# Convolution heads in three passes on high and low halves, with products made ahead in the attention and kept in DRAM

## What is computed

```
x = x + linear_attention(layernorm(x))
# convolution, 32 heads of 8 channels; q = layernorm(x), k = v = ctx
kv  = einsum('bhil,bhjl->bijhl', k_, v_)
y   = irfft(rfft(kv, 2L) * rfft(ssm_kernel, 2L))[..., :L]
out = y + kv * D[None, None, None, :, None]
x = x + einsum('bijhl,bhil->bjhl', out, q_)
x = x + experts(layernorm(x)) + shared_expert(layernorm(x))
```

## Time and profile before

| what | us |
|---|---|
| median of three runs (lowest, highest) | 864.95 (864.42, 866.53) |
| the profiled execution | 864.47 |
| its span, first to last instruction | 861.4 |
| PE busy in the span | 841.6 (98%) |
| DVE, ACT, POOL busy | 544.6, 377.5, 443.2 |
| PE busy from 100 to 140 us (attention) | 39.88 of 40 |
| PE busy from 280 to 320 us (convolution) | 40.00 of 40 |
| POOL busy in the same two stretches | 13.83, 36.52 |

### The profile page before, as it was taken

One profiled execution on the slowest core, in us unless ns is written; L12 is line 12 of the kernel. 1 busy time (PEld: TensorE's weight loads), 2 busy tenths in 40 slices (PEclk: granted clock), 3 DMA queues, 4 the chain that ended last, 5 costly groups with the idle time before them and its releaser, 6 DMA issues.

```text
span 861.4 us, 14213 instructions
## 1 busy us (share of the span) xinstructions
PE 841.6 (98%) x4354; PEld 702.5 (82%) x4354; DVE 544.6 (63%) x850; ACT 377.5 (44%) x608; POOL 443.2 (51%) x436
## 2 busy tenths in 40 slices
PE   8999999999999999999999999999999999999995
PEld 7888888889877777778887788888888888888884
DVE  5767767675657777888769875544455544555431
ACT  5313322333133533442652255555655555655552
POOL 1203223331068899884622343666666666656654
PEclk9999999999999999999999999999999999999998
DMA  8601101100026543440210297988899888999866
GB/s 284 218 25 17 34 24 37 37 12 13 1 62 197 165 129 110 123 132 16 93 63 7 92 322 188 213 207 212 192 190 215 210 210 197 190 199 217 207 120 87
DMA packets 54420, 113.42 MB, mean 132 GB/s; under 512 B 10416, under 2 KB 14256, under 8 KB 54256
## 3 DMA queue, kind: packets, MB, share of 16 engines
q1 hardware_dynamic: 37360, 72.49, 26.3%
q0 software_dynamic: 17024, 40.48, 25.2%
HBM read 82.28 MB, written 30.66 MB: 131 GB/s over the span
## 4 chain that ended last, share of the span: by engine, by line
PE 88%; DVE 6%; issue 2%; DMA 1%; POOL 1%; ACT 1%; POOLq 0%; SPq 0%; DVEq 0%; ACTq 0%
PE PS L206 20%; PE PS L208 20%; PE PS L207 20%; PE PS L217 17%; PE PS L1642 4%; PE PS L704 2%; PE PS L695 2%; PE PS L633 1%; PE PS L1579 1%; PE PS L1569 1%; DMA QY<-in_kwT 1%; PE PS L1578 1%; PE PS L1561 1%; DVE C_halves L1854 1%; DVE prod_halves L1865 1%
## 5 line engine op out<-in xcount | busy, mean ns | idle before, releaser
L206 PE MATMUL PS<-QY_rounded,wh 128*128 128x512 f32 (+1 forms) x376 | 153.2, 407 | 0.0
L208 PE MATMUL PS<-QY_rounded,wl 128*128 128x512 f32 (+1 forms) x376 | 145.7, 387 | 0.0
L1360 POOL DMA_INDIRECT out_y<-QY,idy x72 | 114.4, 1589 | 44.0 <-ACT QY L1451 32.8
L207 PE MATMUL PS<-QY_rounded,wh 128*128 128x512 f32 (+1 forms) x312 | 120.1, 385 | 0.0
L1911 DVE TENSOR_TENSOR hTl<-hh,hTh 128x512 fp32r<-128x512 f32 (+1 forms) x39 | 27.5, 705 | 107.6 <-ACT hTh L1432 107.6
L1337 POOL DMA_INDIRECT xg<-xs_d,idx x64 | 77.0, 1204 | 28.8 <-issue 14.2
L208 PEld LDWEIGHTS PS<-QY_rounded,wl 128*128 128x128 f32 x376 | 70.6, 188 | 15.1
L217 PE MATMUL PS<-qER,Tz 128*128 128x288 f32 x320 | 81.1, 407 | 0.5 <-DVE QY L1062 0.4
L217 PE MATMUL PS<-prod,Tz 128*128 128x288 f32 x320 | 80.5, 406 | 0.2 <-DVE term L1045 0.2
L206 PEld LDWEIGHTS PS<-QY_rounded,wh 128*128 128x128 f32 x376 | 71.0, 189 | 11.0
L1451 ACT ACTIVATE QY<-PS,WPOS 128x512 f32<-128x512 f32 x76 | 52.4, 690 | 55.0 <-PE PS L208 55.0
(11 more groups left out here) (237 smaller groups left out, 1907.5 us busy)
## 6 DMA issues: line engine op xcount, KB each, us to landing
ws<-in_gu_w SPq DMA_DIRECT2D x38, 512.0 KB, 5.5
ws<-in_dn_w SPq DMA_DIRECT2D x20, 512.0 KB, 6.6
C<-in_ctx SPq DMA_DIRECT2D x32, 256.0 KB, 2.6
Tz<-kpad_d SPq DMA_DIRECT2D x32, 256.0 KB, 3.3
xs_d<-xn SPq DMA_DIRECT2D x16, 256.0 KB, 2.0
out_y<-X SPq DMA_DIRECT2D x16, 256.0 KB, 7.2
X<-in_x SPq DMA_DIRECT2D x1, 3072.0 KB, 18.0
xn<-in_xT SPq DMA_DIRECT2D x5, 512.0 KB, 3.2
```

Source lines behind the costliest of these rows:

```text
L206: pe.matmul(out_, lh, rh, start=first, stop=False)
L207: pe.matmul(out_, lh, rl, start=False, stop=False)
L208: return pe.matmul(out_, ll, rh, start=False, stop=last)
L1360: nc.gpsimd.indirect_dma_start(out=out, out_offset=bass.IndirectOffsetOnAxis(ap=idy[:, t:t + 1], axis=0), in_=yo[:, t], in_offset=None, co ...
```

## The change

The 15 odd heads from 3 to 31 run as `three_pass` on high and low halves (head 1 and the 16 even ones stay fp32).
- Their products are made on GpSimd in the attention, three sets in each of the five rounds (`products_ahead`): one set after `rstd(0, b + 1)`, two after the four `xz` steps and before `rstd(1, b - 1)`. A set is three instructions (512, 512 and 128 elements) from C2[1] into prod[0]. SyncE stores each to `prod_d` in DRAM (576 KB) and loads the next context into C2[1] behind the store; the next set waits for both to land. `products(0, 0)` comes after the fifteenth store.
- The padded kernel is split on GpSimd into halves as well, in the tiles aTh and aTl, and stored (`kpad_hl_d`); ScalarE waits for these stores before its step 1.
- In the convolution SyncE loads an odd head's products into one tile `odd` (576 KB) once the low half of the head before is made, and the two Toeplitz halves (256 KB each) into two buffers. ScalarE makes the high half (`odd_high`), GpSimd the low one (`odd_low`, 1152 elements), each into two buffers. GpSimd no longer makes products for k = 1, and TensorE's `convolve_halves` waits for `odd_lo`, the halves and the banks.
- `shared_lo` moves from GpSimd (three steps of 1024) to VectorE (six of 512, one at the end of each of the pairs 6 to 11).
- Semaphores of the weights' high and low parts are merged into `w_hi` and `w_lo`; some hardware loops are unrolled or stepped by two; eight warm-up passes before the last transposes read WH instead of aTl.

```diff
@@ -68,6 +71,8 @@
         kpad_d = nc.dram_tensor("kpad_d", (CH, KPAD + 1), F32).ap()
+        kpad_hl_d = nc.dram_tensor("kpad_hl_d", (2, CH, KPAD + 1), F32).ap()
+        prod_d = nc.dram_tensor("prod_d", (CH // 2, P, DC * B * NPAIR), F32).ap()
         stat_d = nc.dram_tensor("stat_d", (S, 2), F32).ap()
...
@@ -191,7 +199,7 @@
-            pool.wait_ge(c2_in[k], 16 * (i + 1))
+            pool.wait_ge(c2_in[k], 16 * (i + 1) if k == 0 else 16 * (CH // 2))
             pool.wait_ge(conv_ps[k], DC * i)
@@ -257,27 +265,41 @@
             sp.dma_start(kpad_d, kpad[:]).then_inc(kpad_out, 16)
-            sp.wait_ge(kpad_out, 16)
+            for j in range(2):
+                sp.wait_ge(kpad_done, j + 2)
+                sp.dma_start(kpad_hl_d[j], kpad_hl[j].bitcast(F32)).then_inc(kpad_out, 16)
+            sp.wait_ge(kpad_out, 16 * KPADS)
+            load_context(sp, 3, 1)
+            load_context(sp, 0, 0)
             for k in range(2):
-                load_context(sp, k, k)
                 load_toeplitz(sp, k, k)
-            sp.wait_ge(prod_done[0], 2)
-            load_context(sp, 2, 0)
-            with sp.Fori(DIRECT, B) as b:
+
+            def store_products(m):
+                sp.wait_ge(ahead_done, 3 * m)
+                sp.dma_start(prod_d[bass.ds(m, 1)].rearrange("o p n -> p (o n)"), prod[0][:].rearrange("p c b n -> p (c b n)")
+                             ).then_inc(kpad_out, 16)
+
+            def turned_batch(b):
                 sp.wait_ge(xT_lo, TPB * b)
...
                 sp.dma_start(mr, bass.AP(tensor=stat_d.tensor, offset=0, ap=[[0, P], [2 * P, TPB], [1, 2 * P]])).then_inc(xt_mr_in, 16)
-            sp.wait_ge(prod_done[1], 2)
-            load_context(sp, 3, 1)
-            sp.wait_ge(conv_ps[0], DC)
-            load_toeplitz(sp, 2, 0)
-            sp.wait_ge(prod_done[0], 4)
-            load_context(sp, 4, 0)
-            sp.wait_ge(conv_ps[1], DC)
-            load_toeplitz(sp, 3, 1)
+
+            with sp.Fori(DIRECT, B - 1) as b:
+                turned_batch(b)
+                for j in range(AHEAD):
+                    m = b * AHEAD + (j + 1 - DIRECT * AHEAD)
+                    store_products(m)
+                    sp.dma_start(C2[1][:], ctx2[bass.ds(m * 2 + 3, 1)].rearrange("o p c b j -> p (o c b) j")).then_inc(c2_in[1], 16)
+            turned_batch(B - 1)
+            for j in range(AHEAD):
+                m = (B - 1 - DIRECT) * AHEAD + j + 1
+                store_products(m)
+                load_context(sp, 2 * m + 3 if m < CH // 2 - 1 else 1, 1)
+            sp.wait_ge(prod_done[0], 2)
+            load_context(sp, 2, 0)
@@ -304,12 +326,30 @@
             nc.gpsimd.tensor_tensor(kpad[:, P - 1:P], kpad[:, P - 1:P], dsk[:], ALU.add).then_inc(kpad_done, 1)
-            wait_apart(pool, kpad_out, 16)
-            products(pool, 0, 0)
+            pool.wait_ge(kpad_done, 1)
+            nc.gpsimd.tensor_copy(kpad_hl[0], kpad[:]).then_inc(kpad_done, 1)
+            wait_apart(pool, q_ps, 1)
+            pool.wait_ge(kpad_done, 2)
+            nc.gpsimd.tensor_tensor(kpad_hl[1], kpad[:], kpad_hl[0].bitcast(F32), ALU.subtract).then_inc(kpad_done, 1)
             rstd(pool, 0, 2)
             rstd(pool, 1, 0)
+
+            def products_ahead(m):
+                pool.wait_ge(c2_in[1], 16 * m)
+                wait_apart(pool, kpad_out, 16 * (KPADS - 1) + 16 * m)
+                o = prod[0][:].rearrange("p c b n -> p (c b) n")
+                a = C2[1][:]
+                for half in range(2):
+                    shifted = bass.AP(tensor=a.tensor, offset=a.offset + 2 * half, ap=[a.ap[0], a.ap[1], [1, 2], [1, CD]])
+                    nc.gpsimd.tensor_tensor(o[:, :, 2 * half * CD:2 * (half + 1) * CD].rearrange("p a (s j) -> p a s j", s=2),
+                                            a[:, :, 0:CD].unsqueeze(2).broadcast_to([P, LB, 2, CD]), shifted,
+                                            ALU.mult).then_inc(ahead_done, 1)
+                nc.gpsimd.tensor_tensor(o[:, :, 4 * CD:], a[:, :, 0:4], a[:, :, 4:8], ALU.mult).then_inc(ahead_done, 1)
+
             with pool.Fori(2, B - 1) as b:
                 rstd(pool, 0, b + 1, mv[0][:, :, 1])
+                m = b * AHEAD + (1 - (DIRECT - 1) * AHEAD)
+                products_ahead(m)
                 wait_apart(pool, xt_mr_in, 32 * (b - 1))
@@ -320,7 +360,11 @@
                                             ALU.mult).then_inc(z_done, 1)
+                for j in range(1, AHEAD):
+                    products_ahead(m + j)
                 rstd(pool, 1, b - 1)
+            wait_apart(pool, kpad_out, 16 * (KPADS + CH // 2 - 1))
+            products(pool, 0, 0)
             pool.wait_ge(qp_done, B)
...
@@ -408,9 +452,10 @@
                 act.wait_ge(wk_in[h], 16)
-                act.activation(WH[:, 1, 2 * h:2 * h + 2], wstage[:, 1, 2 * h:2 * h + 2], ACT.Copy).then_inc(wk_hi, 1)
+                act.activation(WH[:, 1, 2 * h:2 * h + 2], wstage[:, 1, 2 * h:2 * h + 2], ACT.Copy).then_inc(w_hi, 1)
             act.wait_ge(nqb_done, 1)
             step(0, first=True)
+            wait_apart(act, kpad_out, 16 * KPADS)
             step(1)
...
@@ -893,6 +939,10 @@
         term = [sb2(f"term{k}", [P, CD // 2, LB, CD, 2]) for k in range(2)]
+        odd = sb2("odd", [P, DC, B, NPAIR])
+        odd_h, odd_l = ([sb2(f"odd_{n}{k}", [P, DC, B, NPAIR], F32R) for k in range(2)] for n in ("high", "low"))
+
+        TzHi, TzLo = ([sb2(f"Tz_{n}{k}", [P, D]) for k in range(2)] for n in ("high", "low"))
         q2_done, term_behind, reduced = sem("q2_done"), sem("term_behind"), sem("reduced")
@@ -902,18 +952,37 @@
             def _(sp):
+                def load_ahead(m):
+                    if m > 1:
+                        sp.wait_ge(odd_lo, m - 1)
+                    sp.dma_start(odd[:].rearrange("p c b n -> p (c b n)"), prod_d[m]).then_inc(ahead_in, 16)
+
+                def load_toeplitz_halves(m):
+                    for j, dst in enumerate((TzHi[m % 2], TzLo[m % 2])):
+                        src = bass.AP(tensor=kpad_hl_d.tensor, offset=(j * CH + 2 * m + 1) * (KPAD + 1), ap=[[1, P], [1, D]])
+                        sp.dma_start(dst[:], src).then_inc(tzr_in[m % 2], 16)
+
                 def next_heads(i, last=False):
-                    sp.wait_ge(prod_done[1], 2 * (i + 1))
-                    load_context(sp, 2 * i + 3, 1)
+                    load_ahead(i + 1)
                     sp.wait_ge(conv_ps[0], DC * (i + 1))
...
                         load_context(sp, 2 * i + 4, 0)
-                    sp.wait_ge(conv_ps[1], DC * (i + 1))
-                    load_toeplitz(sp, 2 * i + 3, 1)
-
+                        sp.wait_ge(conv_ps[1], DC * (i + 1))
+                        load_toeplitz_halves(i + 2)
+
+                sp.wait_ge(kpad_out, 16 * (KPADS + CH // 2 - 1))
+                sp.wait_ge(v_ps, TPB * B)
+                load_ahead(1)
+                sp.wait_ge(o_ps, TPB * B)
+                load_toeplitz_halves(1)
+                sp.wait_ge(conv_ps[0], DC)
+                load_toeplitz(sp, 2, 0)
+                load_toeplitz_halves(2)
+                sp.wait_ge(prod_done[0], 4)
+                load_context(sp, 4, 0)
                 next_heads(1)
...
@@ -947,28 +1016,28 @@
-                def pair_of_heads(i):
-                    products(pool, i, 1)
+                def odd_low(m, k):
+                    wait_apart(pool, odd_hi, m)
+                    nc.gpsimd.tensor_tensor(odd_l[k][:], odd[:], odd_h[k][:].bitcast(F32), ALU.subtract).then_inc(odd_lo, 1)
+
+                def pair_of_heads(i, k):
                     terms_behind(i - 1, 1)
...
                     terms_behind(i, 0)
+                    odd_low(i + 1, 1 - k)
                 terms_behind(0, 0)
-                pair_of_heads(1)
+                odd_low(1, 1)
+                pair_of_heads(1, 1)
                 nc.gpsimd.memset(zrow[:], 0.0).then_inc(memsets, 1)
-                def shared_lo(a, b):
-                    nc.gpsimd.tensor_tensor(wl[:, a:b], ws[:, a:b], wh[:, a:b].bitcast(F32), ALU.subtract
-                                            ).then_inc(fixed_lo, 1)
-
-                with pool.Fori(2, 6) as i:
-                    pair_of_heads(i)
+                with pool.Fori(2, 6, 2) as i:
+                    for k in range(2):
+                        pair_of_heads(i + k, k)
                 pool.wait_ge(fixed_hi, 3)
                 nc.gpsimd.tensor_tensor(gw_hl[:, :, 1], gw[:], gw_hl[:, :, 0].bitcast(F32), ALU.subtract).then_inc(fixed_lo, 1)
-                for part in range(NG - 1):
-                    pair_of_heads(6 + part)
-                    shared_lo(2 * part, 2 * part + 2)
+                for i in range(6, stream_head(0) // 2):
+                    pair_of_heads(i, i % 2)
                 for i in range(stream_head(0) // 2, CH // 2):
-                    products(pool, i, 1)
                     for e in range(EARLY):
...
@@ -997,10 +1068,19 @@
-                def pair_of_heads(i):
```

(48 more changed lines are left out.)

67 lines of the change are left out of this document (41 added, 26 removed).

## The result

The changed kernel takes 878.2 us against 865.3 us, median of four runs each: 1.015 of the time before, with a 95% interval of 1.0135 to 1.0165. It is slower, and lies outside the forecast range. The profiled execution took 876.95 us with a span of 874.9.

The account below looks back on a forecast made before the run. TensorE was taken as the bound, with 88% of the chain that ended last. 864.47 - 12.75 (passes) + 1.35 (change of kind) + 2.0 (VectorE) + 0.7 (transfers) + 8.3 (attention) = 864.1 us; range 855.5 to 870.5.

Parts of the forecast that it names:

- Part 5: Attention: product sets and their DRAM trip delay the last rstd, 9.05 us gap in five rounds, costing 8.3 us.
- rival (b): Attention, last rstd: loop longer than priced, from 9.8 us a round; 867.8 us, 869.4 with 10.1 us; chance 0.20.
- 1.6 us of slack: Attention: time before TensorE asks for the divided rows ahead of the K projection, deducted once from the delay.
- the rule: Attention: price is the sum of the five gaps before the late rstd, less 35.3 and less 1.6 us.
- Part 1: Convolution, TensorE: odd heads take 4.00 instead of 4.85 us, gaining 12.75 us, with 1.35 back for changes of kind.
- my sign: Convolution, steady pairs: 4.0 to 4.1 us from an odd head's first pass to the next even head's.
- Part 2: Convolution, GpSimd: products, terms and low half take 8.49 us of a pair's 8.95; fits, costed at nothing.
- Part 3: Convolution, pairs 6 to 12: VectorE's six shared low-weight subtractions stall TensorE 2.0 us, bounds 0.5 and 5.
- Part 4: Convolution DMAs: Toeplitz load late once, where 1 MB of shared weights loads; 0.7 us, bounds nothing and 0.7 in 15 pairs.
- Rival (c): Convolution bound by the single Toeplitz buffer: 0.7 us lost in each of 15 pairs, 874 us; chance 0.05.
- rival (d): Convolution, TensorE: three passes cost as much as the fp32 product, no gain, 875.5 us; chance 0.04.
- Rival (a): Attention: round trip cheap or hidden, gap under 7.4 us a round, only the convolution shows; 855.8 us; chance 0.15.

Follow-up runs that it names:

- the kernel with all mends: Changed kernel with last rstd before the third set, shared low halves on GpSimd at the end, shared weights in three loads: 854.1 us, repeated 856.9 us.
- the pieces: Shared weights loaded as 3 x 512 KB behind context loads, against the kernel with rstd moved and low halves on GpSimd at the end: 854.1 us.

## Why the prediction was wrong

The step that failed first is the gap in front of the late rstd, 9.05 us in the forecast and 9.95 measured, because a hold-up that was named was left out of the sum. That alone would have stayed within the range. Two more steps carried the time out of it: TensorE's clock, which no part had, and the stalls of the convolution, which took 8.5 us of its 12.75 (12.75 - 4.29), where the sum had 4.05 (1.35 + 2.0 + 0.7).

**Part 5, the attention: the mechanism held, the gap was too small.** I took 9.05 us a round, it is 9.95 in the mean of five. Two of its terms failed. The set behind the xz steps takes 3.35 us and not 2.47, in each of the rounds, also where no transfer runs; VectorE's two subtractions of two SBUF tiles run at that time and take 2.57 us (1.12 and 0.69 in the earlier trace rows). And the wait for the context is 4.28, not 4.05. (The forecast names no row for the 0.65 to 1.1 us per 256 KB in its trip; the stores of 576 KB landed in 3.1 us in the median, within the 2.8 to 3.4 that it took.) That is 0.9 x 5 = 4.5 us, and would have given 868.6: rival (b) with its own point, 9.8 us. I named the hold-up there, priced it at 0.4 us from the single row, and left it out of the sum. The 1.6 us of slack, once, and the adding up of the delays were right, as the table shows.

**What no part had: the clock.** The forecast took TensorE's clock as 1.00 throughout. Behind a stall of 2 us it can fall to half for some us. In the changed kernel's first profile 2.6 us of the attention's price are over the rule (15.45 less 12.8), and I put them down to it; the table above says how far that is shown. After the convolution more of it: the changed kernel has clocks of 0.84 and 0.73 in the 8 us from 411 on, where the kernel before has 1.00 and so has the kernel with the moved rstd:

```profile
411.00:415.00 4.00, 4.00 (x29) 0.84 0.00 0
415.00:419.00 4.00, 4.00 (x19) 0.73 0.02 4
```

That is 4 x 0.16 + 4 x 0.27 = 1.7 us of the 2.3 us lost there. Which stall set it off is open: the kernel with all mends has such a fall in one profile (0.60 for 4 us) and none in the other.

**Part 1, the passes:** right. A steady pair takes 8.83 us, and the 1.35 us for the change of kind aren't seen; the even head became as much shorter (4.64 us to the next in such a pair, for 4.85) as the odd one is longer than 4.00 (4.19, where my sign was 4.0 to 4.1).

**Part 2, GpSimd in the convolution:** right. The low half takes 2.65 us, forecast 2.63, and the steady pairs keep TensorE's pace. (The lack that I gave for a low half of 3.1 us, 0.05 us a pair, should read 0.01: 8.49 + 0.47 against 8.95.)

**Part 3, VectorE's low parts:** three of the six were held until a GpSimd instruction ended and took 1.71 to 2.15 us, the other three took 0.68 to 0.87, where I took 1.12 for each. Their stall is 2.9 us by the run that moved them, forecast 2.0, bound 5. Part of the miss is arithmetic: a bank that is read out after 3.1 us and wanted back after 4.0 to 4.4 leaves 0.9 to 1.3 us, not the 1.5 that I used, and 3.55 less these is 2.25 to 2.65. The Trainium skill's rule ("SBUF — State Buffer", "Who interferes with whom"), that such instructions exclude each other whole, agrees with the 1.94 us row above. That its price came in under the bound of 5 us I put down to the three that hardly waited and to the slack of one head.

**What Part 3 left out: pairs 11 to 13.** Even with the mends they take 10.44, 10.48 and 10.42 us, and by Part 1 they should take 8.83 plus what the transposes add (0.88, 0.88, 0.44 before): 9.71, 9.71, 9.27. VectorE works in pairs 11 and 12 from one end to the other (7.5 + 1.85 + 0.68 = 10.0 us, and 0.26 to 0.29 us of idle time ahead of each head's terms), and the odd head of pair 13 waits 0.78 us for its last low half. I compared 9.95 with 9.85 and found 0.1 over; the idle times between instructions I had summed at nothing. It is 2.6 us.

**Part 4, transfers:** the place was right (where the 1 MB is loaded), the size wasn't, and pair 15 was missing (0.89 and 1.23 us in the two profiles). I took 0.7 us once; pairs 2 and 3 lose 2 us in the changed kernel's first profile and 4.6 in its second (22.61 against 18.0 with the pieces), with the clock's fall. The Toeplitz load of pair 3 took 5.7 us in the first, forecast up to 4.7. Rival (c), 0.7 us in each pair, didn't come; rival (d) fell with Part 1. With the 2.9 and 2.6 us above, 2.0 for pairs 2 and 3 and 0.9 for pair 15 make 8.4 of the 8.5 us.

**The sum.** 864.1 forecast; 4.5 from the gap, 2.6 from the clock in the attention, 4.4 in the convolution (8.7 forecast, 4.3 gained) and 1.3 after it (2.3 less the 1.0 around the span) make 876.9, which is the profiled time; as the last three are differences of marks, that they add up shows nothing. Each of the four was inside or near a bound I had given, or of a kind I hadn't; all of them had the same sign. The range didn't reach because it let one term go to its end at a time, though the attention's and the convolution's upper bounds share a cause, GpSimd at work beside VectorE.

Rival (a)'s time is what the kernel with the moved rstd comes near, though by another order and not by a cheaper trip: the attention hidden but for 0.6 us, 860.95 us measured for 855.8. Most of the 5 us between are the convolution's, which gained 4.4 us there and not 8.7.

## What to carry to other kernels

Work that is put into an idle engine is free where its place in the queue is in front of nothing that a loop hangs on, or where it fits into the wait that was there (two sets without their trips did): look for the instruction behind it, and put the new work after that, here one line and 17 us. Price a late step by the length of the gap, round by round, with durations read beside the engine that will run then, and let bounds that share a cause go to their ends together. And expect that a TensorE stall of 2 us can cost more than 2 us.

## What the runs showed of the hardware

A VectorE subtraction of two SBUF tiles, 128x512, took from 0.68 to 2.15 us beside GpSimd, and GpSimd's next instruction took 0.90 instead of 0.45 us; a 128x2 `var_eps` on GpSimd took 1.03 instead of 0.22 us behind VectorE's 1.23 us addition of two tiles. TensorE's clock fell to its lower level behind stalls of 2.23, 2.51, 2.56 and 2.93 us in the convolution and not behind 1.87 and 1.98, while in the attention stalls of 1.80 to 2.19 us did it in three profiles (two in each), and others of up to 2.24 us in the same profiles and 2.30 in another of the same code did not; that is open. Passes of 288 columns on halves kept their pitch of 0.133 us between fp32 heads, with no price for the change of kind.
